# A three-layer graph network on one core: the final norm done per node tile inside layer 3, spread relative-source rows double buffered, one sorted-part difference kept in f32, edge attributes loaded once

## What is computed

```python
for k in range(3):
    e = edge_vector @ edge_W[k] + edge_b[k]
    msg = relu(x[src] + e)
    agg = segment_sum(msg, dst, num_segments=n)
    z = (1.0 + eps[k]) * x + agg
    h = relu(batch_norm(z @ W1[k] + b1[k]))
    x = relu(layer_norm(h @ W2[k] + b2[k], ln_g, ln_b))
out = _layernorm(x0 + x)          # (v - mean) / sqrt(var + 1e-5), per node
```

## Time and profile before

| quantity | value |
|---|---|
| median of 3 runs | 1476.94 us |
| the profiled execution | 1472.82 us |
| its span, first to last instruction | 1470.9 us |
| mean granted clock of TensorE | 0.936 |
| TensorE, busy share | 85% |
| VectorE, busy share | 71% |
| GpSimd, busy share | 61% |
| ScalarE, busy share | 40% |

### The profile page before, as it was taken

One profiled execution on the slowest core, in us unless ns is written; L12 is line 12 of the kernel. 1 busy time (PEld: TensorE's weight loads), 2 busy tenths in 40 slices (PEclk: granted clock), 3 DMA queues, 4 the chain that ended last, 5 costly groups with the idle time before them and its releaser, 6 DMA issues.

```text
span 1470.9 us, 37463 instructions
## 1 busy us (share of the span) xinstructions
PE 1256.8 (85%) x13834; PEld 1032.8 (70%) x13834; DVE 1041.0 (71%) x1871; ACT 587.1 (40%) x1157; POOL 896.0 (61%) x842
## 2 busy tenths in 40 slices
PE   2479889899888799889898589999998799999991
PEld 1245445454444688888888589999998689999991
DVE  7776667666877597778888666666666666667667
ACT  0234443443333144334444344444445244444451
POOL 0145556555565777656664277777773777777750
PEclk9699999999999799989999799999999899999995
DMA  7269889988888877666768657777778467777752
GB/s 169 68 219 278 266 282 275 275 282 271 283 250 281 255 232 212 204 203 199 240 195 261 182 155 233 220 214 237 218 222 246 136 208 221 213 226 215 222 160 67
DMA packets 261672, 323.39 MB, mean 220 GB/s; under 512 B 55303, under 2 KB 172089, under 8 KB 261537
## 3 DMA queue, kind: packets, MB, share of 16 engines
q1 hardware_dynamic: 208632, 218.82, 48.7%
q0 software_dynamic: 33280, 82.06, 17.2%
q10 hardware_dynamic: 19625, 20.58, 6.9%
HBM read 213.80 MB, written 107.55 MB: 218 GB/s over the span
## 4 chain that ended last, share of the span: by engine, by line
PE 31%; POOL 17%; DVE 15%; issue 15%; DMA 14%; ACT 3%; ACTq 3%; SPq 1%; DVEq 0%
POOL rows L601 16%; PE ps L1327 12%; DMA rows<-attr_dram 8%; PE ps L1356 4%; PE ps L1346 3%; DVE terms L951 3%; DMA relB<-relrow_dram 3%; PE ps L1297 2%; ACTq L385 2%; PE ps L1298 2%; PE ps L1299 2%; PE ps L1300 2%; PE ps L1301 2%; DVE hot_stage L978 1%; DMA rows<-table_dram,src_i 1%
## 5 line engine op out<-in xcount | busy, mean ns | idle before, releaser
L601 POOL DMA_INDIRECT rows<-table_dram,src_i x416 | 438.4, 1054 | 187.7 <-issue 181.6
L585 POOL DMA_INDIRECT srt_dram<-region,pos_i x208 | 240.1, 1154 | 241.7 <-ACT region L659 193.7
L601 POOL DMA_INDIRECT rows<-x_dram,src_i x208 | 215.4, 1035 | 98.8 <-issue 55.8
L1327 PE MATMUL ps<-xs,early_words 125*128 125x128 bf16 x2720 | 258.3, 224 | 15.9 <-issue 15.9
L1327 PE MATMUL ps<-xs,region 125*128 125x128 bf16 x2584 | 244.5, 224 | 17.7 <-issue 13.8
L1327 PE MATMUL ps<-xr,early_words 125*128 125x128 bf16 x1360 | 248.0, 224 | 0.0
L1327 PE MATMUL ps<-xr,region 125*128 125x128 bf16 x1292 | 234.8, 223 | 0.0
L1327 PEld LDWEIGHTS ps<-xs,early_words 125*128 125x128 fp8e4 x2720 | 222.7, 100 | 16.5 <-issue 16.4
L1327 PEld LDWEIGHTS ps<-xs,region 125*128 125x128 fp8e4 x2584 | 210.8, 100 | 18.2 <-issue 14.1
L1047 DVE TENSOR_TENSOR terms<-ps,terms 128x512 f32<-128x512 f32 x156 | 107.1, 687 | 157.6 <-PE ps L1327 152.1
L1297 PE MATMUL ps<-wf,rows 128*128 128x384 bf16 x416 | 142.1, 342 | 73.4 <-ACT region L655 53.8
(11 more groups left out here) (140 smaller groups left out, 2229.8 us busy)
## 6 DMA issues: line engine op xcount, KB each, us to landing
ep_dram<-terms SPq DMA_DIRECT2D x52, 768.0 KB, 5.4
terms<-srt_dram SPq DMA_DIRECT2D x156, 256.0 KB
terms<-ep_dram SPq DMA_DIRECT2D x156, 256.0 KB
early_words<-hotrow_dram SPq DMA_DIRECT2D x156, 104.0 KB
rows<-attr_dram SPq DMA_DIRECT2D x108, 128.0 KB, 4.2
rows<-attr_dram ACTq DMA_DIRECT2D x100, 128.0 KB
region<-kept_dram SPq DMA_DIRECT2D x13, 576.0 KB
early_words<-kept_dram SPq DMA_DIRECT2D x13, 576.0 KB
```

Of the source, the lines that this page charges most:

```text
L585: pool.indirect_dma_start(srt, bass.IndirectOffsetOnAxis(ap=pos_i[:, c:c + 1], axis=0), stage_s[:, q, t, :], None).then_inc(scattered[q], 16)
L601: pool.indirect_dma_start(rows[:, q, t * FEAT:(t + 1) * FEAT], None, source, bass.IndirectOffsetOnAxis(ap=src_i[:, c:c + 1], axis=0),).the ...
L1327: ins = nc.tensor.matmul(bank(q)[:, c:c + FEAT], hot_g[v % 2][0:SLICE, h, at:at + P], x_part(part, FIRST[t] + k), start=k == 0 and part == ...
```

## The change

- **Final norm.** In layer 3, `features` is dropped on ScalarE. VectorE does, at the end of each body with node tiles, `final_sum` for both tiles: relu and the addition of the input in one instruction, then statistics. ScalarE takes the root (`final_deviation`) where `features` stood. In the next body, after `turn(0)`, VectorE does `final_norm`: reciprocal and normalising, in place in x_cur. SyncE loads the input two tiles at a time (`load_first`) and stores two tiles at a time (`store_out`), between its other loads. The four last tiles follow in `nodes_at_end`.
- **relB** gets a second buffer for each half, and is loaded one body earlier. `build_hots` can be made in two pieces: two of the five instructions of half 0 before `turn(1)`, the other three where they were; two of half 1 before `turn(3)`, three where they were.
- **Parts.** The second difference (L1065) goes to an f32 tile of its own, `last_s`; TensorE reads its high halves.
- **Attributes** are loaded once, to partitions 0 to 63. `split_attr` works on these. `second_part` copies two things to partitions 64 to 127: the high halves of `left` (as before) and, after a wait for L953, the low halves of `whole`. TensorE waits for both.
- **Between layers** the last four tiles' rows are written by SyncE, not by ScalarE; statistics and norm of these tiles alternate on VectorE, root and relu on ScalarE. The first chunk of `split_x` has 8 slices, the second 6.
- VectorE's code of layers 2 and 3 is written out by layer, and that of layer 3 by body; ScalarE's has layer 3 apart.

```diff
-CHUNKS = ((0, 9), (9, 14), (14, SLICES))
+CHUNKS = ((0, 8), (8, 14), (14, SLICES))
...
-            for half in range(2):
-                eng.dma_start(attr_t[half * EDGE_FEAT:(half + 1) * EDGE_FEAT, slot, :],
-                              attr[b * EDGE_FEAT:(b + 1) * EDGE_FEAT, q * QUAD * P:(q + 1) * QUAD * P]
-                              ).then_inc(attr_loaded[slot], 16)
+            eng.dma_start(attr_t[0:EDGE_FEAT, slot, :],
+                          attr[b * EDGE_FEAT:(b + 1) * EDGE_FEAT, q * QUAD * P:(q + 1) * QUAD * P]
+                          ).then_inc(attr_loaded[slot], 16)
...
             def load_rel(j, h):
 
-                if j >= 1:
-                    sp.wait_ge(hot_here[(j - 1) % 2][h], 16 * ((j - 1) // 2 + 1))
+                if j >= 2:
+                    sp.wait_ge(hot_here[j % 2][h], 16 * (j // 2))
...
+            def load_first(j):
+
+                t = 2 * j - 4
+                if j >= 4:
+                    sp.wait_ge(fin_added, t - 2)
+                sp.dma_start(x_first[:, j % 2, :, :], x[t * NT:(t + 2) * NT, :].rearrange("(t p) d -> p t d", p=NT)
+                             ).then_inc(x_first_loaded[j % 2], 16)
...
+                        if l == LAYERS - 1 and j >= 2 and q == 1:
+                            load_first(j)
+                        if l == LAYERS - 1 and j >= 5 and q == 2:
+                            store_out(j - 3)
...
                     if l >= 1 and j == 0:
+                        for t in range(NODE_TILES - TAIL, NODE_TILES):
+                            sp.wait_ge(x_ready, node(l - 1, t) + NODE_TILES)
+                            sp.dma_start(tables[l - 1][t * NT:(t + 1) * NT, :], x_cur[:, t, :]).then_inc(table_ready, 16)
...
-                    slot = 2 * kind + n % 2
-                    act.wait_ge(attr_rest, 2 * n + kind + 1)
-                    nc.scalar.activation(high(attr_t[EDGE_FEAT:P, slot, :], QUAD * P),
-                                         high(attr_r[EDGE_FEAT:P, kind, :], QUAD * P), ACT.Copy).then_inc(attr_mid, 1)
+                    slot, m = 2 * kind + n % 2, 2 * n + kind
+                    top, bottom = attr_t[0:EDGE_FEAT, slot, :], attr_t[EDGE_FEAT:P, slot, :]
+                    act.wait_ge(attr_rest, m + 1)
+                    nc.scalar.activation(high(bottom, QUAD * P), high(attr_r[0:EDGE_FEAT, kind, :], QUAD * P),
+                                         ACT.Copy).then_inc(attr_mid, 1)
+                    act.wait_ge(attr_low, m + 1)
+                    nc.scalar.activation(low(bottom, QUAD * P), low(top, QUAD * P), ACT.Copy).then_inc(attr_mid, 1)
...
-                nc.vector.tensor_tensor(low(whole, n), left, high(left, n), ALU.subtract).then_inc(s_parts, 1)
+                nc.vector.tensor_tensor(last, left, high(left, n), ALU.subtract).then_inc(s_parts, 1)
...
+            def final_sum(t, h, loaded, slot):
+
+                dve.wait_ge(x_first_loaded[slot], loaded)
+                dve.wait_ge(norm_ready, node(LAYERS - 1, t))
+                nc.vector.scalar_tensor_tensor(one(x_cur, t), norm[:, h, :], 0.0, x_first[:, slot, h % 2, :],
+                                               ALU.max, ALU.add).then_inc(fin_added, 1)
+                dve.wait_ge(fin_added, t + 1)
+                nc.vector.bn_stats(stats[:, TAIL + h, :], one(x_cur, t)).then_inc(fin_stats, 1)
+                dve.wait_ge(fin_stats, t + 1)
+                nc.vector.bn_aggr(mean_var[:, TAIL + h, :], stats[:, TAIL + h, :]).then_inc(fin_var, 1)
+
+            def final_norm(t, h):
+
+                dve.wait_ge(fin_std, t + 1)
+                nc.vector.reciprocal(rstd[:, TAIL + h:TAIL + h + 1], std[:, TAIL + h:TAIL + h + 1]).then_inc(fin_rstd, 1)
+                dve.wait_ge(fin_rstd, t + 1)
+                dve.wait_ge(fin_var, t + 1)
+                nc.vector.tensor_scalar(one(x_cur, t), one(x_cur, t), mean_var[:, TAIL + h, 0:1],
+                                        rstd[:, TAIL + h:TAIL + h + 1], ALU.subtract, ALU.mult).then_inc(fin_ready, 1)
...
                 turn(0)
+                if final == "later":
+                    final_norm(j * 2 - 6, 0)
+                    final_norm(j * 2 - 5, 1)
                 if flushes:
                     flush(l, j - 1, 0, first=flushes == "first")
                     flush(l, j - 1, 1)
+                if builds and not last:
+                    build_hots(j + 1, 0, 0, 2)
                 turn(1)
...
                 if builds and not last:
-                    build_hots(j + 1, 0)
+                    build_hots(j + 1, 0, 2)
...
                 turn(2)
+                if builds and not last:
+                    build_hots(j + 1, 1, 0, 2)
                 turn(3)
...
                 if builds and not last:
-                    build_hots(j + 1, 1)
+                    build_hots(j + 1, 1, 2)
                 if nodes:
                     node_norm(l, *a, b[0])
                     node_norm(l, *b, b[0])
+                if nodes and final:
+                    slot, loaded = visit
+                    final_sum(*a, loaded, slot)
+                    final_sum(*b, loaded, slot)
```

More of the change, by code:

```diff
@@ L352, in build @@
         end_step = sem("end_step")
+        x_first_loaded = [sem(f"x_first_loaded{slot}") for slot in range(2)]
+        fin_added = sem("fin_added")
+        fin_stats = sem("fin_stats")
+        fin_var = sem("fin_var")
+        fin_std = sem("fin_std")
+        fin_rstd = sem("fin_rstd")
+        fin_ready = sem("fin_ready")
         last_var = sem("last_var")
@@ L500, in _ @@
                     if j == REL_BODY:
-                        for h in range(2):
-                            load_rel(0, h)
+                        for body in range(2):
+                            for h in range(2):
+                                load_rel(body, h)
                 for n in range(2):
@@ L745, in _, with layer @@
                         staged(j, q)
-                with act.Fori(0, LAYERS) as l:
+                def layer(l, final):
                     wait_alone(act, "act", x_ready, (l + 1) * NODE_TILES)
@@ L752, in _ @@
                     with act.Fori(2, BODIES - 1) as j:
-                        body(l, j, True)
-                    body(l, BODIES - 1, True, last=True)
+                        body(l, j, True, final=final)
+                    body(l, BODIES - 1, True, last=True, final=final)
                     first = NODE_TILES - TAIL
@@ L1058, in parts @@
                 at = quad(l, j, q)
-                whole, left = terms[:, q, :], rest_s[:, q % 2, :]
+                whole, left, last = terms[:, q, :], rest_s[:, q % 2, :], last_s[:, q % 2, :]
                 n = QUAD * FEAT
@@ L1180, in _ @@
                 nodes_at_end(0)
-                with dve.Fori(1, LAYERS) as l:
+                for l in range(1, LAYERS):
                     split_x(l)
@@ L1186, in _ @@
                     body(l, 1, "first", False, False)
-                    with dve.Fori(2, BODIES - 1) as j:
-                        body(l, j, True, True, False)
-                    body(l, BODIES - 1, True, True, False, last=True)
-                    nodes_at_end(l)
+                    if l < LAYERS - 1:
+                        with dve.Fori(2, BODIES - 1) as j:
+                            body(l, j, True, True, False)
+                        body(l, BODIES - 1, True, True, False, last=True)
+                        nodes_at_end(l)
+                    else:
+                        for j in range(2, BODIES):
+                            body(l, j, True, True, False, last=j == BODIES - 1, final="first" if j == 2 else "later",
+                                 visit=(j % 2, 16 * (j // 2)))
+                        nodes_at_end(l, True)
             with dve.Else():
@@ new lines, in last_norm @@
+                def last_norm(g, ts):
+                    dve.wait_ge(last_std, g + 1)
+                    ending(nc.vector.reciprocal(rstd[:, ts], std[:, ts]))
+                    for t in range(ts.start, ts.stop):
+                        ins = nc.vector.tensor_scalar(result[:, t, :], x_in[:, t, :], mean_var[:, t, 0:1], rstd[:, t:t + 1],
+                                                      ALU.subtract, ALU.mult)
+                    ins.then_inc(out_ready, 1)
+                for g, ts in enumerate(groups()):
+                    last_stats(ts)
+                    if g >= 1:
+                        last_norm(g - 1, groups()[g - 1])
@@ L1273, in _ @@
+                last_norm(GROUPS - 1, groups()[-1])
         @block.tensor
@@ L1344, in scatter_s @@
                 for t in range(QUAD):
-                    for part in (high(whole, QUAD * FEAT), high(left, QUAD * FEAT), low(whole, QUAD * FEAT)):
+                    for part in (high(whole, QUAD * FEAT), high(left, QUAD * FEAT), high(last, QUAD * FEAT)):
                         ins = nc.tensor.matmul(ps[:, bass.ds(col, SORT_WINDOW)], part[:, t * FEAT:(t + 1) * FEAT],
```

176 lines of the change are left out of this document (106 added, 70 removed).

## The result

The changed kernel takes 1436.46 us (median of 4 runs, 1433.21 to 1441.65), the kernel before 1478.75 beside it (4 runs, 1475.05 to 1481.23): a ratio of 0.9732, 95% interval 0.9702 to 0.9761. That is faster, and 8 us above the forecast of 1428. The profiled execution takes 1436.87 us, 36.0 less than before; its span is 1435.1 us, 35.8 less.

A forecast was written before the change was run, and what follows sets the result against it. It took layer 2 as bound by TensorE and GpSimd, layer 1 by TensorE's stall on ScalarE, staging by a ring of engines. 30 + 2 + 4 - 2 + 15 = 49 off 1472.8 gives 1424, plus 4.1: 1428 us (1412 to 1442).

The forecast's parts named there:

- Layer 1: Layer 1: earlier relB load and moved builds cut a body from 25.8 to 22.7 us, minus 30 in all.
- The bound of 38: Layer 1: the most it could gain, 38 us, set by GpSimd's gathers.
- the term for the split: Layer 1: two of five builds leave the stretch between gather and norm, 1.23 us a body.
- makes (13.9 + 17.6) / 4 = 7.9 us a quad: Staging: second ring's time for a plain pair of quads plus a pair with hots_of, against 8.0 before.
- the ring: Staging: second ring of emptying, split, L655 behind four copies and 40 matmuls; two quads go from 13.0 to 13.9 us.
- Its own sign of being wrong: Staging: the forecast would be wrong if a quad took 8.5 us.
- within 10 us of before: Staging: its total length expected to stay this close to the kernel before.
- The other side of the sum: Staging: single attribute load, with fewer issues and bytes, shortens the first ring by 0.1 to 0.7 us a quad.
- Rival 1: Staging grows by part of the copies' 0.9 us: 0.5 a quad, plus 25 for minus 2, 1455; chance 0.14.
- Rival 2: ScalarE becomes the staging's limit, copies paid whole at 1.56 us a quad, plus 81, 1511; chance 0.04.
- Rival 4: Layer 3: VectorE locks GpSimd out during the added normalising, up to plus 12 us, 1440; chance 0.05.
- Rival 3: Layer 1: builds only change places, stall stays, only relB's wait is gained, 7 us, 1451; chance 0.09.

The follow-up runs named there:

- e5: Changed kernel with the two halves' builds whole again, where they stood before, relB still double; 1452.00 us, ratio 0.9818.
- e4: Changed kernel with relB single again, loaded where it was before, builds still in two pieces; 1519.72 us, ratio 1.0255.
- e12: Changed kernel with 40 matmuls into unused columns where TensorE stood idle, once in four staging quads; 1425.07 us, ratio 0.9698.
- e2: Changed kernel with the second load of each quad's attributes kept, the four copies and their waits staying; 1446.75 us, ratio 0.9845.
- e1: Changed kernel with the staging of before: attributes loaded twice, split on 128 partitions, two copies a quad; 1424.19 us, ratio 0.9703.
- e6: Changed kernel with ScalarE's plain-way attribute copies behind emptying L694, and the load for quad n+2 behind those copies; 1411.87 us, ratio 0.9600.
- e7: Changed kernel with the boundaries between layers as before, including a first split_x chunk of 9 slices; 1436.28 us, ratio 0.9703.
- e9: Changed kernel with the final norm as before: after layer 3, in seven groups, with features in layer 3; 1453.02 us, ratio 0.9806.
- e10: Changed kernel with the second difference written to the low halves in bf16 again, not to the f32 tile; 1437.52 us, ratio 0.9706.
- e3: Changed kernel with ScalarE's plain-way attribute copies behind emptying L694 and the load for quad n+2; 1409.89 us, ratio 0.9601.
- e8: e3 with the two instructions of hots_of two quads apart; 1395.15 us, ratio 0.9424.

## Why the prediction came out as it did

**The total: right, with some luck.** 1436 lies in the forecast range, but only 36 of the 49 us came off the profiled execution, 13 too few. That the median is just 8 off is chance: the prediction added 4.1 for the distance of the kernel before's median from its profiled execution, and the changed kernel's median lies 0.4 below its own. The missing 13 are the staging's 15 and small differences elsewhere.

**Layer 1: as argued.** The forecast body was 22.7, it is 22.67; what is left of TensorE's stall was put at 0.9 us a body and is 3.6 / 10 = 0.4, and the other 0.4 in which TensorE is idle lies in other waits, so the exact hit is in part luck. The bound of 38 doesn't follow from the numbers beside it: 25.8 less 21.4, for ten bodies, is 44. e5 bears out the term for the split. What the prediction missed is that the two terms are not independent: it priced the second buffer at the 0.7 us of wait that it removes, and e4 shows that with the split it carries 49 + 32 = 81 us of layer 1, because the wait that it prevents isn't the one in the trace of before.

**Staging: the step that failed** is "makes (13.9 + 17.6) / 4 = 7.9 us a quad". Its mechanism, that L655, now L694, stands behind four copies, is right, and so are both prices of the ring at full clock: 13.8 measured for the plain pair, and 17.5 for the other one in e12. But it took 6.95 us for 40 matmuls in every quad, and behind the 3.1 to 3.9 us of idle time 20 of them run at 1.2 GHz. Over the staging that is 183.3 - 177.2 = 6.1 ns for each of 52 x 40 matmuls, 12.7 of the 13.3 us (an estimate, which takes all of it to be on the path). Its own sign of being wrong, a quad of 8.5, was nearly met with 8.36, and "within 10 us of before" was missed. Rows 1 had the 0.97 on record, and I took the clock for a constant. The other side of the sum was also right in kind. By the same estimate, between e2 and the changed kernel the clock takes 183.3 - 177.7 = 5.6 ns x 2080 = 11.6 us; with these put back, the single load is worth 9.9 + 11.6 = 21.5 us or 0.41 a quad (forecast 0.1 to 0.7), and the copies cost 0.4 of the 0.9. That they cancel is measured by e12 against the kernel before, 485.2 and 485.1. ScalarE's sequencer handed the load on as forecast: at 261.99, ahead of the emptying that it follows in the program, at 262.67. Rival 1 had the sign, and twice the price. Its cause is half of it: the copies do cost 0.4 a quad (e2 against e1), but without the clock's fall the single load pays for them (e12). Rival 2 (all of the copies' 81 us on the path) fell with the result, and e6 shows the load's place to be worth nothing.

**Between layers: -4 forecast, about -1 measured.** From the first tail statistics to GpSimd's gather it was 10.37 and 9.39 us, and is 10.33 and 8.58; in e7, 10.78 and 9.41. Over all kernels with the new order it is 9.42 to 10.88 at the first boundary, which tells nothing, and 8.18 to 9.22 at the second, under both values of the old one. The timeline of ScalarE's last relu, SyncE's stores and GpSimd, first boundary, then the second:

```profile
812.43 0.31 ACT L747 ACTIVATE x_cur<-region 121x128 f32<-121x128 f32 x1 [0.40 <-DVE region L1165]
...
811.77 1.67 SPq L561 DMA_DIRECT2D table_dram<-x_cur  x4
...
817.59 0.94 POOL L637 DMA_INDIRECT rows<-table_dram,src_i  x1 [35.76 <-DMA table_dram<-x_cur]
```

```profile
1120.40 3.81 SPq L561 DMA_DIRECT2D table_dram<-x_cur  x4
...
1126.21 0.94 POOL L637 DMA_INDIRECT rows<-table_dram,src_i  x1 [24.66 <-issue]
```

The relu is early, as forecast: it starts 5.2 us after the first tail statistics, at the second boundary 5.9, before 7.6. But the gather starts 4.2 us after the issue of the last store has ended at the first boundary, 2.0 at the second; behind ScalarE's last store it was 2.0 as well (833.78 plus 0.31 to 836.08). At the first, SyncE had issued loads of four other tiles on the same queue from 809.91 to 811.30. The prediction asked what stands behind the stores, and not what stands ahead of them. That these loads are the cause was not tried.

**Final norm: -15 forecast; -18 in the tail and (e9) -15 to -17 in the whole measured.** The tail runs 11.0 us where I had 11.2; the error is in its start, put 2.1 us later for the `final_sum` of tiles 20 and 21. Layer 3 up to the tail takes 295.7 us on the mean of twelve kernels with the new norm (293.2 to 298.3) and 294.6 and 292.7 in the two with the old: some 2 us longer, the forecast's +2, but within the scatter.

**f32 difference: 0, and 0 measured** (697 ns instead of 757, e10). **Rival 4** falls: GpSimd's gathers take 1.022 us in layer 3 (115.51 / 113) beside VectorE's added instructions, 1.031 in layer 2 without them. The means of the earlier trace rows hide a small effect of the builds, though. In layer 1, gathers that run beside a build for over 0.5 us have a median of 1.02 us in the kernel before (64 of 208) and 1.08 in the changed kernel (57), those beside none 0.94 and 0.95. That is 0.08 and 0.13 us, far from a build's whole length of 0.6 to 0.7; whether the builds are its cause was not tried. **Rival 3** falls with e5.

## What to carry to other kernels

Price a longer wait of TensorE twice: its own length, and the matmuls behind it, if they then come at half the clock; look in the trace for the spacing of matmuls behind the longest idle stretches, not for the mean clock of a stage. When a buffer is doubled and a consumer moved forward in the same change, the wait seen before the change prices neither. And a copy that seems free because its engine has idle time isn't, if it stands in a queue ahead of what another engine waits for: two of the same four copies, put behind the emptying, made the same staging 25 us shorter, and moving VectorE's side work apart another 16.

## What the hardware showed

- TensorE behind 3.1 to 3.9 us without a matmul: up to 20 matmuls of 384 columns 0.32 us apart in place of 0.17 (clock 0.52). Behind 2.0 to 2.5 us: 0.17 in some places, 0.25 on the mean of the next 20 in others, in the same kernel (e3, the kernel before); behind the 1.3 us that e8 has in its place, 0.17 each time.
- Forty matmuls of 128 columns, 2.46 us, in the place of idle time kept the matmuls behind them at 0.17 us, that is at 2.4 GHz, and made the staging 13 us shorter (e12).
- Fewer bytes did not hold the clock up: with four copies and two loads a quad it was 0.97 (e2), with one load 0.92. From 163 to 417 us e2 has one idle stretch of TensorE of over 3 us, the changed kernel nine.
- In e4, whose TensorE waits some 6 us a body for L729 (41.2 us in seven waits from 580 to 800 us), the clock there was 0.87, in the changed kernel's ten bodies 0.99. Some of the 81 us may be this; how much was not measured.
